# State weighing, layer-norm statistics and masks moved between engines in a two-layer transformer kernel on one core

## What is computed

```
h = layernorm(x) * (1 + ca) + sa
x = x + ga * attention(h)            # 16 heads, causal, ALiBi bias
h = layernorm(x) * (1 + cb) + sb
x = x + gb * fp4_ffn(h)              # blockwise fp4, silu(gate) * up, down
h = layernorm(x) * (1 + ca) + sa     # second layer
x = x + ga * state_space(h)          # below, with a layer norm of its own
h = layernorm(x) * (1 + cb) + sb
x = x + gb * experts(h)              # base + shared + 2 of 6 routed

# state_space: 512 channels, 16 states per channel
dA = exp(dt * A)                     # one factor per token, channel, state
h  = dA * h + (dt * u) * B           # recurrence over 1024 tokens
y  = sum over the states of h * C
y  = (y + u * D) * silu(z);  out = y @ W_out.T + residual
```

## Time and profile before

| | us |
|---|---|
| median of 3 runs (4206.35 to 4210.94) | 4210.48 |
| the profiled execution | 4207.32 |
| its span, first to last instruction | 4205.4 |
| VectorE busy | 3592.4 (85%) |
| TensorE busy | 3374.6 (80%) |
| GpSimd busy | 2620.3 (62%) |
| ScalarE busy | 2249.4 (53%) |

### The profile page before, as it was taken

The page is one execution under the profiler, slowest core; times in us unless marked ns, Lnnn a source line. Parts: engine busy times, 40 slices in busy tenths (PEclk is TensorE's granted clock), DMA queues, the critical chain, the costliest instruction groups (busy, mean ns, idle before and its releaser), DMA issues. The chain is left out here.

```text
span 4205.4 us, 60689 instructions
## 1 busy us (share of the span) xinstructions
PE 3374.6 (80%) x21452; PEld 1522.8 (36%) x21452; DVE 3592.4 (85%) x6348; ACT 2249.4 (53%) x3974; POOL 2620.3 (62%) x2515
## 2 busy tenths in 40 slices
PE   5979999999994999999567777777777777777467
PEld 3623333333332555565222222222222222222166
DVE  5768888888855999999289999999999999999966
ACT  5626666666672333333265665666665565665422
POOL 1102322222222888887188888988889898988823
PEclk8969999999996999999778887888888888887689
DMA  4884565656513111110112222222222222212122
GB/s 146 279 175 67 75 88 67 88 75 82 77 32 87 35 44 47 47 43 26 47 48 52 69 59 62 67 58 50 54 69 60 66 65 56 67 51 52 40 93 83
DMA packets 273931, 299.55 MB, mean 71 GB/s; under 512 B 34559, under 2 KB 204662, under 8 KB 273622
## 3 DMA queue, kind: packets, MB, share of 16 engines
q1 hardware_dynamic: 273630, 295.68, 31.7%
HBM read 210.22 MB, written 84.51 MB: 70 GB/s over the span
## 5 line engine op out<-in xcount | busy, mean ns | idle before, releaser
L1679 POOL TENSOR_TENSOR d_dBu<-d_dtu,d_Bn 128x1024 f32<-128x1024 f32 x512 | 1202.7, 2377 | 157.7 <-DVE d_h L1746 157.5
L1525 ACT ACTIVATE d_dA<-d_dt,d_decay 128x512 f32<-128x512 f32 x1024 | 688.6, 687 | 414.2 <-DVE d_h L1746 412.5
L745 ACT ACTIVATE b_P<-b_pT 128x512 f32<-128x512 f32 (+1 forms) x1120 | 571.4, 576 | 328.8 <-PE b_pT L653 328.5
L1746 DVE TENSOR_TENSOR_SCAN d_h<-d_dA,d_last_h,d_dBu 128x512 f32<-128x512 f32 x512 | 616.9, 1265 | 21.2 <-ACT d_dA L1525 18.2
L1746 DVE TENSOR_TENSOR_SCAN d_h<-d_dA,d_dBu 128x512 f32<-128x512 f32 x512 | 587.1, 1205 | 50.3 <-ACT d_dA L1525 47.9
L775 DVE CUSTOM_DVE_ANT_0 b_pS<-b_pS,mask_qk 128x512 f32<-128x512 f32 (+3 forms) x1024 | 581.2, 618 | 50.1 <-PE b_pS L663 45.1
L663 PE MATMUL b_pS<-KS,QS 99*128 99x512 bf16 (+3 forms) x1536 | 471.4, 339 | 71.7 <-DVE b_Gc L775 47.3
L625 POOL TENSOR_SCALAR_AFFINE_SELECT b_P<-b_P 128x128 f32<-128x128 f32 (+2 forms) x608 | 191.4, 321 | 506.1 <-ACT b_P L745 493.3
L653 PE MATMUL b_pT<-QS,KS 118*128 118x512 bf16 (+3 forms) x1536 | 450.1, 330 | 19.5 <-ACT b_gT L729 16.3
L1753 DVE TENSOR_TENSOR d_h<-d_h,d_C 128x2048 f32<-128x2048 f32 x192 | 434.6, 2263 | 0.5 <-PE d_C L1408 0.5
L1408 PE MATMUL d_C<-d_bc,d_pick 96*128 96x512 bf16 x256 | 118.0, 461 | 359.5 <-DVE d_h L1753 359.2
(11 more groups left out here) (300 smaller groups left out, 5906.5 us busy)
## 6 DMA issues: line engine op xcount, KB each, us to landing
d_Bn<-scratch_bs SPq DMA_DIRECT2D x64, 1024.0 KB, 8.2
scratch_parts<-a_part SPq DMA_DIRECT2D x48, 512.0 KB, 4.1
QS<-scratch_parts SPq DMA_DIRECT2D x192, 128.0 KB, 7.3
KS<-scratch_parts SPq DMA_DIRECT2D x192, 128.0 KB, 7.8
scratch_v<-a_v SPq DMA_DIRECT2D x16, 1024.0 KB, 7.6
V<-scratch_v SPq DMA_DIRECT2D x32, 512.0 KB, 11.7
a_x<-in_L_attn_x_dram SPq DMA_DIRECT2D x16, 512.0 KB, 7.6
scratch_o<-b_O SPq DMA_DIRECT2D x16, 512.0 KB, 10.2
```

The costliest lines, as they stand in the source:

```text
L745: act.activation(t[:, heads[0]:heads[-1] + 1, c * CH:c * CH + w], pT[:, place % RING, 0:len(heads) * w].rearrange("p (h w) -> p h w", w=w) ...
L1525: act.activation(dA[:, m % 2, :], dt[:, c.k % 2, m, :], ACT.Exp, scale=decay[:, m, n:n + 1]).then_inc(dA_d, 1)
L1679: pool.tensor_tensor(dBu[:, n % 2, 2 * j:2 * j + 2, :], dtu[:, c.k % 2, 2 * j:2 * j + 2, :], Bn[:, n // BG % 2, n % BG, :].unsqueeze(1).to ...
L1746: dve.tensor_tensor_scan(h[:, n % HS, m, :], dA[:, m % 2, :], dBu[:, n % 2, m, :], start, ALU.mult, ALU.add).then_inc(scanned, 1)
```

## The change

1. **feed_forward takes the statistics of its result.** Two roles are added to the pipeline, s at lag 10 and v at lag 11. ScalarE sums x2 of a tile (Copy with an accumulator), makes the negative mean over 16, and sums the squares of (x2 - mean) / 16 (Square with an accumulator), into `x2_neg` and `x2_var`, one column for each of 64 tiles. In `state_space` GpSimd makes scale and bias for all 64 tiles at the start of the block (two additions or products, one power and one product over 64 columns). VectorE's statistics of x at place 1 go, and so does `scale_bias` at place 3; ScalarE's first `normalise` waits for these 64 columns and for the load of x.
2. **Products over whole states.** One instruction over 2048 columns per state in place of two over 1024, in three buffers in place of two; the product of state n needs all scans of state n - 3. VectorE waits for the whole product before its first scan. B is loaded two states at a time (`BG` = 2), twice as many DMAs of half the size in the same order among SP's other work.
3. **Five states on GpSimd.** `POOL_C` = 0, 3, 6, 9, 12; VectorE weighs eleven states in place of twelve.
4. **The fourth inner projection** goes behind the state sums of its place on TensorE; ScalarE's `inner(q, 3)` goes from the second half of place 1 to the first part of place 2.
5. **Masks in attend.** The affine_select on the diagonal pieces becomes a tensor_tensor on GpSimd, a product in int32 of the bits with a 0/1 triangle `cap` that setup makes. The value of the edge rows goes from -1e30 to -1024.

```diff
-                pool.affine_select(out=own, in_=own, compare_op=ALU.is_ge, fill=0.0,
-                                   base=0, pattern=[[0, len(heads)], [-1, P]], channel_multiplier=1).then_inc(p_masked, 1)
+                pool.tensor_tensor(own.bitcast(I32), own.bitcast(I32), K["cap"][:, :].unsqueeze(1).to_broadcast([P, len(heads), P]), ALU.mult).then_inc(p_masked, 1)
...
-        LAGS = LAG_E, LAG_N, LAG_D, LAG_B, LAG_H, LAG_Q, LAG_C, LAG_O = 1, 2, 3, 5, 6, 7, 8, 9
+        LAGS = LAG_E, LAG_N, LAG_D, LAG_B, LAG_H, LAG_Q, LAG_C, LAG_O, LAG_S, LAG_V = 1, 2, 3, 5, 6, 7, 8, 9, 10, 11
...
+                if v_ is not None:
+                    n = v_.base * U + v_.k
+                    wait(act, sum_d, v_.times(1, 1))
+                    act.activation(K["x2_neg"][:, n:n + 1], x2_sum[:, n % 2, :], ACT.Copy, scale=-1.0 / (16.0 * D)).then_inc(neg_d, 1)
...
+                if v_ is not None:
+                    n = v_.base * U + v_.k
+                    wait(act, neg_d, v_.times(1, 1))
+                    act.activation(unread[:, n % 2, :], x[:, n % XS, :], ACT.Square, bias=K["x2_neg"][:, n:n + 1], scale=1.0 / 16.0, accum_out=K["x2_var"][:, n:n + 1]).then_inc(var_d, 1)
+                if s_ is not None:
+                    n = s_.base * U + s_.k
+                    wait(act, x2_d, s_.times(1, 1))
+                    wait(act, var_d, s_.times(1, -1))
+                    act.activation(unread[:, n % 2, :], x[:, n % XS, :], ACT.Copy, accum_out=x2_sum[:, n % 2, :]).then_inc(sum_d, 1)
...
-POOL_C = (0, 4, 8, 12)
+POOL_C = (0, 3, 6, 9, 12)
...
-HS, BG = 4, 4
+HS, BG, BS = 4, 2, 3
...
+            def spread_next(c, g):
+
+                if c is not None:
+                    wait(sp, dBu_d, c.times(NS, BG * (g - 1)))
+                    spread_b(c, g)
...
-                 {1: lambda q: project(q, IN + 3, 3),
-                  2: lambda q: convolve(q, 0), 3: lambda q: convolve(q, 1), 4: lambda q: convolve(q, 2), 5: lambda q: convolve(q, 3),
+                 {2: lambda q: convolve(q, 0), 3: lambda q: convolve(q, 1), 4: lambda q: convolve(q, 2), 5: lambda q: convolve(q, 3),
...
-                 {0: lambda q: project(q, IN + 2, 2), 7: project_x, 8: lambda q: project_dt(q, 1), 9: lambda q: project_dt(q, 3),
+                 {0: lambda q: project(q, IN + 2, 2), 1: lambda q: project(q, IN + 3, 3), 7: project_x, 8: lambda q: project_dt(q, 1), 9: lambda q: project_dt(q, 3),
...
-                for j in range(2):
-                    wait(pool, scanned, c.times(NS * MD, MD * (n - 2) + 2 * j + 2))
-                    pool.tensor_tensor(dBu[:, n % 2, 2 * j:2 * j + 2, :], dtu[:, c.k % 2, 2 * j:2 * j + 2, :],
-                                       Bn[:, n // BG % 2, n % BG, :].unsqueeze(1).to_broadcast([P, 2, CH]), ALU.mult).then_inc(dBu_d, 1)
+                wait(pool, scanned, c.times(NS * MD, MD * (n + 1 - BS)))
+                pool.tensor_tensor(product(c, n), dtu[:, c.k % 2, :, :], Bn[:, n // BG % 2, n % BG, :].unsqueeze(1).to_broadcast([P, MD, CH]), ALU.mult).then_inc(dBu_d, 1)
...
+            pool.tensor_tensor(rstd_x[:, :], K["x2_var"][:, :], eps[:, :], ALU.add).then_inc(sx_step, 1)
+            pool.tensor_tensor(nmr_x[:, :], K["x2_neg"][:, :], sixteen[:, :], ALU.mult).then_inc(sx_step, 1)
+            pool.wait_ge(sx_step, 2)
+            pool.tensor_tensor(rstd_x[:, :], rstd_x[:, :], half[:, :], ALU.pow).then_inc(sx_step, 1)
+            pool.wait_ge(sx_step, 3)
+            pool.tensor_tensor(nmr_x[:, :], nmr_x[:, :], rstd_x[:, :], ALU.mult).then_inc(sx, 1)
...
-                    if m % 2 == 0:
-                        wait(dve, dBu_d, c.times(2 * NS, 2 * n + m // 2 + 1))
+                wait(dve, dBu_d, c.times(NS, n + 1))
...
-                 {1: lambda f: stats(f, 0), 4: modulate, 6: lambda f: stats(f, 1), 13: carry}))
+                 {4: modulate, 6: stats, 13: carry}))
```

141 lines of the change are left out of this document (76 added, 65 removed).

## The result

The changed kernel takes 4222.95 us (median of 11 runs, 4216.12 to 4227.14), the kernel before beside it 4208.47 us (11 runs, 4205.03 to 4214.61): ratio 1.0029, 95% interval 1.0020 to 1.0038. It is slower by 12.2 us by that ratio (14.5 by the two medians) where the prediction said 25.6 us faster. The profiled execution spans 4221.2 us, 15.8 more than before, at a granted clock of 0.884 (before 0.881).

What follows compares the result with a forecast made beforehand. VectorE was taken to pace state_space, TensorE attend, and both to fill feed_forward. Terms -54 + 7.6 + 20.3 + 0.5 = -25.6 took the profiled 4207.3 to 4181.7, as a median 4185; forecast 4165 to 4204 (chance 0.52), 8-in-10 range 4145 to 4226.

Steps and rivals of the forecast that it cites:

- attend, 20.3: In attend, GpSimd's int32 mask product delays TensorE at block 3 by 0.635 us in 32 units: 20.3 us more.
- setup, 0.5: In setup, one more memset and select: 0.5 us more.
- feed_forward, 0: In feed_forward, ScalarE's two added activations, 1.2 to 1.6 us, fit under 2.06 us of cover: nothing added.
- The power, 7.6: At state_space's start, GpSimd's power over 64 columns takes 10.4 us and delays the first normalise: 7.6 us more.
- state_space, -54: In state_space, VectorE gains 6.98 us a chunk and 3.6 comes back: net 3.4, over 16 chunks 54 us less.
- statistics: In state_space, VectorE no longer takes the statistics of x: 1.78 us a chunk less.
- wait for y: In state_space, VectorE's wait before gating y goes once the state sum precedes the fourth projection: 2.94 us a chunk less.
- the wait at scan 15: In state_space, VectorE waits for GpSimd's whole product of state 15: 2.0 us a chunk more.
- my 0.9 and 0.2 a chunk: In state_space, GpSimd holds up VectorE's product with 1 + ca by 0.9 us and its split of C by 0.2.
- my 0.5 a chunk: In state_space, ScalarE's dA comes later without the cover of VectorE's weighing of state 9: 0.5 us a chunk (0 to 2).
- state_space gives its gain back: Rival: GpSimd late at more places, or state 15's sum still waits; state_space gains 10 to 25, total 4205 to 4222; chance 0.14.
- The rule of the Trainium skill: VectorE instructions with two SBUF inputs and GpSimd's SBUF reads exclude each other: net 2 a chunk, total 4207.

Runs made afterwards that it cites:

- f2: Changed kernel with affine_select masks, the power in two steps (4 and 60 columns) and four states on GpSimd: 4167.67 us against 4213.73 for the kernel before, ratio 0.9896.
- e2: Changed kernel with four states on GpSimd (0, 4, 8, 12) in place of five: ratio 0.9975 to the kernel before, 22.7 us less than the changed kernel.
- j3: Changed kernel with the gate's four projections on TensorE cut to one of two matmuls: ratio 0.9976 to the kernel before, 22.3 us less than the changed kernel.
- j1: Four states on GpSimd, affine_select masks, power in two steps, and VectorE's weighing of state 9 cut to one column: ratio 0.9877 to the kernel before.
- j2: Changed kernel with ScalarE's two long activations for dt cut from 2048 to 32 columns: ratio 0.9945 to the kernel before, 35.4 us less than the changed kernel.
- h2: Changed kernel with GpSimd's weighing of state 9 cut to one column in place of 2048: ratio 1.0015 to the kernel before.
- j4: Changed kernel with ScalarE's two dt activations cut to 32 columns and the gate's four projections to one matmul: ratio 0.9895 to the kernel before.
- e5: Changed kernel with the power for x's scale and bias in two steps, four columns first, then 60: ratio 1.0016 to the kernel before.

## Why the prediction was wrong

Point by point, against the predicted sum of -54 + 7.6 + 20.3 + 0.5 = -25.6:

- **attend, 20.3, and setup, 0.5: right.** Measured 21.4 up to feed_forward; the products run at the float rate that I took (0.726 and 1.269 us for 256 and 512 columns).
- **feed_forward, 0: right within 1.0 us.** The stretch from its first load to its last store is 687.0 for 686.0. Each of the two activations takes 0.40 and 0.49 us and each read of an accumulator 0.19, so 1.27 us in all, under the cover of 2.06.
- **The power, 7.6: right at its place** (7.4 up to the first normalise; 10.56 us for 64 columns, 10.4 forecast). The 3.4 more that were lost before the first scan are two projections of TensorE at the lower clock, as shown above. I had not looked at the fill of the pipeline, where no other chunk hides such a thing.
- **state_space, -54: this failed; measured -17.9 in the recurrence.** It has two parts, and f2 tells them apart, since its recurrence has all of the change but the fifth state. By my own terms, statistics, wait for y and the wait at scan 15 make 16 x (1.78 + 2.94 - 2.0) = 43.5 us less, and f2's recurrence is 47.8 us under that of before (1820.9 for 1868.7). That part was right in its sum, with some luck: the statistics and the wait for y brought 65.9 us and not 75.5 (see the slips below), scan 15 cost 34.1 for 32, and 16 us of small waits and holds-up went that I had not counted. The fifth state makes 16 x (2.26 - 0.9 - 0.2 - 0.5) = 10.6 us less by my terms.
- **The step that failed is this one, that moving a fifth weighing from VectorE to GpSimd is a gain.** It costs: the recurrence of the changed kernel is 29.9 us over f2's, and by e2 the whole kernel is 22.7 us over the one with four states. VectorE's account for it, f2 to after: the weighing takes off 35.7 us of work, but its busy time falls by only 5.0, so 30.7 us are instructions that are longer or overlap less (my 0.9 and 0.2 a chunk make 17.6), and 34.9 us are waits (my 0.5 a chunk makes 8).
- **The longer instructions.** The split of C is 13.7 us longer than in f2 (0.93 us a chunk over the kernel before, for 0.2 forecast: my order of events had GpSimd's product ending there, and it ended 2 us later). The product with 1 + ca is 8.3 longer than in f2, where it is not held up at all (0.3 a chunk over before, for 0.9). The small copy of 12 columns (8 of them, 468 to 1559 ns from before to after) I did not have at all.
- **The waits.** ScalarE's dA was in its range: before scans 10 and 11 VectorE waits 12.3 us more than in f2, 0.8 a chunk for my 0.5 (0 to 2). What I had at nothing is TensorE: with states 10 and 9 summed at place 12, C of state 12 comes late, ScalarE is blocked and dA behind it. Before scans 13 and 14 that is 13.6 us, and j3, which shortens TensorE's list there, takes 19.0 off the recurrence. Another 13.4 us before scan 4 and the output of place 6 came with the five states, for dA and for the state sums and the output projection of TensorE, and 4.8 before scan 9, now for a product, while 6.3 went before scan 7. I did not take these apart.
- **Why the weighing was worth so little on VectorE:** j1 takes it away and leaves all other lists alone, and keeps 8 us of 36. The rest comes back as waits for dA (62.9 for 35.7 us), 21.8 of them before scan 11. There ScalarE makes dA around its two activations of 1.99 us, and the weighing was the cover for them; j2, which shortens these two, has no wait left there.
- **Smaller slips of the sum.** I took the wait for y in 16 chunks, where the earlier trace rows has 14 of it (41.1 us, not 47), and the statistics in 16, of which two chunks lie before the first scan. So in the recurrence 61.4 us of work and 41.1 of waiting went, 102.5 in place of 112. VectorE's whole account from before to after: 61.4 less work, 28.3 longer or less overlapped, 41.1 less waiting for y and 56.3 more of other idle time (products 40.6, state sums 9.6, output 6.7, the rest under 1): -17.9. So 84.6 us came back, where I had 58.
- **Scan 15** was right in size (2.30 for 2.0) and in its chain. It came with the whole products and not with the fifth state: f2 has 34.1 us there, the changed kernel 34.4.
- The rival *state_space gives its gain back* had the outcome (slower by what attend and the power cost) and a part of the reason. It named GpSimd late at more places by its load and by the blocking. h2 rules out the time of the fifth weighing, and the only new wait for a product beside scan 15 is 6.8 us before scan 9; but the blocking (split of C, product with 1 + ca, copy) was 26 us in the recurrence over the kernel before. The rest was on TensorE and ScalarE.
- The rule of the Trainium skill that I had weighed (SBUF — State Buffer, "Who interferes with whom") agrees with the split of C and the product with 1 + ca, as the ends of these instructions show (last section). The copy has one input, and that rule as I weighed it does not speak of it. The gain of 2 a chunk that it gave, 32 us, was nearer than my 3.4, and its total of 4207 still 16 too low.

What stays open: what the waits before scan 4 and at place 6 hang on, how much of j4's gain the kernel before would have too, and what sets the granted clock in a run. The last one also blurs the price of the fifth state: e2 and f2 have the same lists in the recurrence, and their profiles differ by 16 us there, at a granted clock of 0.876 and 0.884 over the run. From e2's trace alone the fifth state would cost 14.2 us in the recurrence and not 29.9; its sign is the same.

## What to carry to other kernels

Here an instruction taken off the busiest engine was worth 8 us of 36. It is worth its time only if the engines that feed it can go faster at that very place; ask what they do under its cover, and read it from their lists around it, not from their sums. Where the pace is a hand-off between four engines, a wait that is removed tends to come back one place further on (scan 15 to scan 0), and parts of a change can't be priced one at a time. The fill of the pipeline had its own critical path and needs its own sum, the clock of TensorE included.

## What the runs showed of the hardware

- An int32 product on GpSimd took what a float product took: 726 ns for 256 columns, where the float one took 727; for 128 and 512 columns it took 455 and 1269. The affine_select took 406 and 635 for 256 and 512.
- GpSimd's power went by the column: 1.02 us for 4, 9.93 for 60, 10.56 for 64.
- VectorE's split of C, with two SBUF inputs, ended 0.54 to 0.55 us after the end of an instruction of GpSimd in every chunk but the first of before, after and h2, whether it took 1.4 or 2.7 us; in the first chunk GpSimd was idle and it took 0.68. The product with 1 + ca ended 1.08 us after one, in all 14 chunks of the recurrence before and after; in f2, where no instruction of GpSimd ended during it, it took 1.22. The other way round GpSimd's product took 5.50 us in place of 4.53 beside VectorE's product with 1 + ca:

```profile
3117.69 5.50 POOL L1712 TENSOR_TENSOR d_dBu<-d_dtu,d_Bn 128x2048 f32<-128x2048 f32 x1
```

- A copy on VectorE from SBUF to SBUF was held up too, though it has one input: each of the 8 copies of 12 columns ended 0.03 to 0.04 us after the end of an instruction of GpSimd, before and after; they took 468 ns in the mean before and 1559 after.
- TensorE's clock: the same four matmuls took 1.96 us at a granted clock of 1.00 and 3.75 at 0.50. Work that came 2 us earlier in e5 met the lower level and gained nothing.
- An accumulator on a ScalarE activation was an instruction of its own, 186 ns, behind the activation (400 ns for a copy of 256 columns, 494 for a square).
